# Aggregating x before the weights product: x stationary, the adjacency streamed 512 nodes wide, four tiles normed at once

## Chip, cores and metric

The kernel runs on one core of one Trainium2 chip. The metric is the device time of that core in microseconds (us); lower is better. Engines are named as in the profile: PE is TensorE (PEld its weight loads), DVE VectorE, ACT ScalarE, POOL GpSimd, SP the queue that issues most DMAs.

## What is computed

`x` is 4096 x 256, `adj` 4096 x 4096 (mostly zeros, with a full diagonal), `weight` 256 x 256, `t` one number, all fp32.

```python
support = x @ weight
g = (1.0 - t[0]) * support + t[0] * (adj @ support)
out = _layernorm(x + g, axis=-1)
```

Both kernels keep fp32 accuracy by splitting each operand into a high part (a copy rounded to the type fp32r) and a low part (the rest), and adding three products: high by high, high by low, low by high.

## The kernel before

**Support first.** x comes transposed in 16 chunks of 256 nodes (`x_raw`, a ring of 4). ACT makes `x_hi` (L168), POOL `x_lo` (L215). PE takes x as stationary and W as moving operand, 256 columns at a time: 6 matmuls for each of 32 tiles of 128 nodes, 192 in all (L331, L336, L341), into `s_ps`. ACT copies the result to the first 256 columns of `S[:, tile]` (L173) and DVE writes the rest to the last 256 (L247), so that S holds high and low side by side for all 4096 nodes.

**Aggregation.** The 32 output tiles go in 16 pairs. For a tile the transposed adjacency comes in two 1 MB chunks of 16 blocks (`a_raw`, a ring of 4). ACT makes `a_hi` (L180) and DVE `a_lo` (L253), 2048 elements a partition each. For each of the 32 blocks PE runs two matmuls with the adjacency block as the stationary operand: `a_hi` against all 512 columns of S (L361), and `a_lo` against its first 256 (L366). That is 1024 matmuls of each kind.

**Norm.** POOL forms `base` = (1 - t) S + x for a pair in three operations (L220, L223, L231). For each tile DVE adds both halves of `agg` to it (L260, L263) and takes statistics (L266, L270), ACT the root (L184), and DVE the reciprocal with one Newton step and `normed` (L274 to L287). The result is stored per tile.

**Order.** All engines run their own list in order and meet by semaphores. ACT: two `a_high`, then `root` of a tile. DVE: two `a_low`, then `layernorm`. SP: four `load_adj`, each after the `a_low` that frees its slot, `load_rows`, two stores. PE waits for `a_lo_ready` of a chunk, and for `y_ready` of the tile that used its accumulator before. The first matmul of the aggregation needs `S`.

Of the kernel before, what the change touches and what calls it, by code (L numbers as in the profile page):

```python
# [7 lines left out]
CHUNK_BLOCKS = 16  # L19
RING = 4  # L20
X_TILES = 2
X_RING = 4
# [3 lines left out]
def at_start(n):  # L26

    return isinstance(n, int) and n == 0

def gnn_layernorm_kernel(nc, xT, x, adjT, t, W, out):
# [3 lines left out]
    nodes, feats = x.shape  # L35
    TILES = nodes // P
    KT = feats // P
    CHUNK = CHUNK_BLOCKS * P
    PER_TILE = TILES // CHUNK_BLOCKS
    PAIRS = TILES // 2  # L40
    X_CHUNKS = TILES // X_TILES
    S_ROUNDS = X_CHUNKS // X_RING
    assert PER_TILE == 2 and RING == 2 * PER_TILE and S_ROUNDS <= RING

    ctx = ExitStack()
    with ctx:
# [9 lines left out]

# [3 lines left out]
        x_raw = sb("x_raw", [P, X_RING, KT, X_TILES * P])  # L60
        x_hi = sb("x_hi", [P, X_RING, KT, X_TILES * P], f32r)
        x_lo = sb("x_lo", [P, X_RING, KT, X_TILES * P], f32r)
        S = sb("S", [P, TILES, 2 * feats], f32r)
        a_raw = sb("a_raw", [P, RING, CHUNK])
        a_hi = sb("a_hi", [P, RING, CHUNK], f32r)
        a_lo = sb("a_lo", [P, RING, CHUNK], f32r)
        t_col = sb("t_col", [P, 1])
        omt_col = sb("omt_col", [P, 1])
        x_rows = sb("x_rows", [P, 2, feats])
        base = sb("base", [P, 2, feats])  # L70
        s_sum = sb("s_sum", [P, 2, feats])
        s_scaled = sb("s_scaled", [P, 2, feats])
        y_part = sb("y_part", [P, feats])
        y = sb("y", [P, feats])
        stats = sb("stats", [P, 6])
        mean_var = sb("mean_var", [P, 2])
        var_eps = sb("var_eps", [P, 1])
        std = sb("std", [P, 1])
        rstd0 = sb("rstd0", [P, 1])
        newton_q = sb("newton_q", [P, 1])  # L80
        newton_c = sb("newton_c", [P, 1])
        rstd = sb("rstd", [P, 1])
        normed = sb("normed", [P, 2, feats])

        s_ps = [ctx.enter_context(nc.psum_tensor(f"s_ps{i}", [P, X_TILES, feats], f32)) for i in range(X_RING)]
        agg = [ctx.enter_context(nc.psum_tensor(f"agg{i}", [P, 2 * feats], f32)) for i in range(2)]

        w_loaded, t_loaded = sem("w_loaded"), sem("t_loaded")  # L90
        w_hi_ready, w_lo_ready = sem("w_hi_ready"), sem("w_lo_ready")
        omt_ready = sem("omt_ready")
        x_loaded = sems("x_loaded", X_RING)
        x_hi_ready, x_lo_ready = sems("x_hi_ready", X_RING), sems("x_lo_ready", X_RING)
        s_acc_ready = sems("s_acc_ready", X_RING)
        s_hi_ready = sems("s_hi_ready", X_RING)
        s_lo_ready = sems("s_lo_ready", X_RING)
# [3 lines left out]
        rows_loaded = sem("rows_loaded")  # L101
        s_sum_ready, s_scaled_ready, base_ready = sem("s_sum_ready"), sem("s_scaled_ready"), sem("base_ready")
        y_part_ready = sem("y_part_ready")
        y_ready = sems("y_ready", 2)
        stats_ready, mean_var_ready = sem("stats_ready"), sem("mean_var_ready")
        var_eps_ready, std_ready, rstd0_ready = sem("var_eps_ready"), sem("std_ready"), sem("rstd0_ready")
        newton_q_ready, newton_c_ready = sem("newton_q_ready"), sem("newton_c_ready")
# [4 lines left out]

        @block.sync
        def _(sp):
            def load_x(chunk, slot):
                sp.dma_start(x_raw[:, slot], xT[bass.ds(chunk, 1)].rearrange("c p k n -> p (c k) n")
                             ).then_inc(x_loaded[slot], 16)

            def load_adj(chunk, slot):  # L120
                sp.dma_start(a_raw[:, slot], adjT[bass.ds(chunk, 1)].rearrange("c p n -> p (c n)")
                             ).then_inc(a_loaded[slot], 16)

            def load_rows(pair):
                sp.dma_start(x_rows[:, :, :], x[bass.ds(pair * (2 * P), 2 * P)].rearrange("(u p) f -> p u f", p=P)
                             ).then_inc(rows_loaded, 16)

            def store(pair, u):
                sp.wait_ge(normed_ready, pair * 2 + (u + 1))
                sp.dma_start(out[bass.ds(pair * (2 * P) + u * P, P)], normed[:, u]).then_inc(stored[u], 16)  # L130

            for slot in range(X_RING):
                load_x(slot, slot)
            sp.dma_start(t_col[:, :], t.partition_broadcast(P)).then_inc(t_loaded, 16)
            for r in range(1, S_ROUNDS):
                for slot in range(X_RING):
                    sp.wait_ge(x_lo_ready[slot], r)
                    load_x(r * X_RING + slot, slot)
                load_adj(r - 1, r - 1)
            for slot in range(S_ROUNDS - 1, RING):  # L140
                load_adj(slot, slot)
            load_rows(0)

            def refill(pair):
                for slot in range(RING):
                    sp.wait_ge(a_lo_ready[slot], pair + 1)
                    load_adj(pair * RING + (RING + slot), slot)
                sp.wait_ge(base_ready, pair + 1)
                load_rows(pair + 1)

            refill(0)
            with sp.Fori(1, PAIRS - 1) as pair:
                refill(pair)
                store(pair - 1, 0)
                store(pair - 1, 1)
            for pair in (PAIRS - 2, PAIRS - 1):
                store(pair, 0)
                store(pair, 1)
            for u in range(2):
                sp.wait_ge(stored[u], 16 * PAIRS)  # L160

        @block.scalar
        def _(act):
            def x_high(rnd, slot):
                act.wait_ge(x_loaded[slot], 16 * (rnd + 1))

                nc.scalar.activation(x_hi[:, slot], x_raw[:, slot], ACT.Copy).then_inc(x_hi_ready[slot], 1)  # L168

            def s_high(rnd, slot):  # L170
                act.wait_ge(s_acc_ready[slot], rnd + 1)
                tile = (rnd * X_RING + slot) * X_TILES
                nc.scalar.activation(S[:, bass.ds(tile, X_TILES), 0:feats], s_ps[slot][:, :, :], ACT.Copy  # L173
                                     ).then_inc(s_hi_ready[slot], 1)

            def a_high(rnd, slot):
                act.wait_ge(a_loaded[slot], 16 * (rnd + 1))
                if not at_start(rnd):
                    act.wait_ge(a_used[slot], rnd)
                nc.scalar.activation(a_hi[:, slot], a_raw[:, slot], ACT.Copy).then_inc(a_hi_ready[slot], 1)  # L180

            def root(tile):
                act.wait_ge(var_eps_ready, tile + 1)
# [3 lines left out]
            x_high(0, 0)  # L187
            act.wait_ge(w_loaded, 16)
            nc.scalar.activation(w_hi[:, :, :], w_raw[:, :, :], ACT.Copy).then_inc(w_hi_ready, 1)  # L189
            for slot in range(1, X_RING):  # L190
                x_high(0, slot)
            with act.Fori(0, S_ROUNDS - 1) as rnd:
                for slot in range(X_RING):
                    s_high(rnd, slot)
                    x_high(rnd + 1, slot)
            a_high(0, 0)
            for slot in range(X_RING):
                s_high(S_ROUNDS - 1, slot)
            for slot in range(1, RING):
                a_high(0, slot)  # L200
            with act.Fori(0, PAIRS - 1) as pair:
                for u in range(2):
                    a_high(pair + 1, 2 * u)
                    a_high(pair + 1, 2 * u + 1)
                    root(pair * 2 + u)
            root(TILES - 2)
            root(TILES - 1)

        @block.gpsimd  # L210
        def _(pool):
            with pool.Fori(0, S_ROUNDS) as rnd:
                for slot in range(X_RING):
                    pool.wait_ge(x_hi_ready[slot], rnd + 1)
                    nc.gpsimd.tensor_tensor(x_lo[:, slot], x_raw[:, slot], x_hi[:, slot].bitcast(f32), ALU.subtract  # L215
                                            ).then_inc(x_lo_ready[slot], 1)

            def make_base(pair):
                s_pair = S[:, bass.ds(pair * 2, 2), :].bitcast(f32)
# [8 lines left out]
                if not at_start(pair):  # L228
                    for u in range(2):
                        pool.wait_ge(y_ready[u], pair)  # L230
# [12 lines left out]
        def _(dve):  # L243
# [57 lines left out]
            for slot in range(1, RING):  # L301
                a_low(0, slot)
# [100 lines left out]
```

## Time and profile before

| | |
|---|---|
| median of 3 runs | 399.12 us (398.97 to 399.54) |
| span of the profiled execution | 397.6 us |
| what lies around the span, by these two | 1.5 us |
| PE busy | 384.0 us, 97% |
| DVE, ACT, POOL busy | 69%, 47%, 22% |
| HBM traffic | 80 MB, 201 GB/s over the span |

The profiled execution's own total is not shown apart from its span, so that the median stands in for it. A busy share is an average over the stages. PE is busy when a matmul is in it; ends of matmuls are modelled, so the spacing of starts is the better measure of what one costs.

### The profile page before, as it was taken

Reading aid. Unit: us, or ns where it says so; the run is one execution under the profiler, and the core shown is the slowest. Engines: PE = TensorE matmul, PEld = TensorE weight load, DVE = VectorE, ACT = ScalarE, POOL = GpSimd, SP = SyncE. Lnnn points to the kernel's source line nnn. Section 1 sums busy time; section 2 is a strip of 40 time slices with the busy share of each in tenths; the row PEclk is TensorE's granted clock in tenths of the full one; section 3 lists DMA queues with packets and bytes.
Section 4 is the critical chain, followed back from the end, with each engine's and each line's share of the span. In section 5 each row is a group of like instructions: output and inputs, shape, how many; then the busy total and the mean of one; then the engine's idle time right before and its main releaser. Section 6 shows DMA issues by size and latency. Waiting matters only on the chain.

```text
span 397.6 us, 6141 instructions
## 1 busy us (share of the span) xinstructions
PE 384.0 (97%) x2240; PEld 336.6 (85%) x2240; DVE 273.1 (69%) x402; ACT 185.1 (47%) x160; POOL 87.9 (22%) x68
## 2 busy tenths in 40 slices
PE   4989999999999999999999999999999999999994
PEld 3978888888888888888888888888888888888883
DVE  1438977777676767777676767777676767777622
ACT  5669535445452635445353635445353635445200
POOL 5765923030300203030200303030200303030100
PEclk9999999999999999999999999999999999999998
DMA  6996966675554665676554665675554664670000
GB/s 185 309 305 222 343 233 235 219 250 211 209 205 170 240 223 176 208 257 211 203 205 176 238 220 176 213 257 211 201 207 176 232 226 172 218 257 13 0 26 13
DMA packets 20900, 80.02 MB, mean 201 GB/s; under 512 B 2208, under 2 KB 10656, under 8 KB 12704
## 3 DMA queue, kind: packets, MB, share of 16 engines
q1 hardware_dynamic: 20624, 79.70, 57.0%
q10 hardware_dynamic: 272, 0.26, 0.2%
q8 instruction: 3, 0.05, 0.0%
q14 instruction: 1, 0.01, 0.0%
HBM read 75.76 MB, written 4.19 MB: 201 GB/s over the span
## 4 chain that ended last, share of the span: by engine, by line
PE 91%; DMA 4%; ACT 2%; DVE 2%; POOL 1%; issue 1%; ACTq 0%; DVEq 0%
PE agg L361 60%; PE agg L366 30%; DMA x_raw<-in_xT 4%; ACT x_hi L168 1%; POOL x_lo L215 1%; DVE a_lo L253 1%; ACT a_hi L180 0%; DVE w_lo L291 0%; PE s_ps L336 0%; ACT S L173 0%; PE s_ps L341 0%; ACT w_hi L189 0%; DVE y_part L260 0%; DVE y L263 0%; DVE stats L266 0%
## 5 line engine op out<-in xcount | busy, mean ns | idle before, releaser
L361 PE MATMUL agg<-S,a_hi 128*128 128x512 f32 x1024 | 356.4, 396 | 0.4 <-DVE a_lo L253 0.4
L366 PE MATMUL agg<-S,a_lo 128*128 128x256 f32 x1024 | 280.3, 279 | 0.0
L361 PEld LDWEIGHTS agg<-S,a_hi 128*128 128x128 f32 x1024 | 189.9, 188 | 44.0 <-DVE a_lo L253 0.6
L253 DVE TENSOR_TENSOR a_lo<-a_raw,a_hi 128x2048 fp32r<-128x2048 f32 x64 | 150.6, 2358 | 70.3 <-ACT a_hi L180 70.3
L366 PEld LDWEIGHTS agg<-S,a_lo 128*128 128x128 f32 x1024 | 192.9, 188 | 2.8
L180 ACT ACTIVATE a_hi<-a_raw 128x2048 fp32r<-128x2048 f32 x64 | 122.2, 1913 | 67.8 <-PE agg L361 67.7
L231 POOL TENSOR_TENSOR base<-s_scaled,x_rows 128x512 f32<-128x512 f32 x16 | 22.6, 1411 | 272.2 <-DVE y L263 272.1
L184 ACT ACTIVATE std<-var_eps 128x1 f32<-128x1 f32 x32 | 6.5, 203 | 126.1 <-DVE var_eps L272 126.1
L287 DVE TENSOR_SCALAR normed<-y,mean_var,rstd 128x256 f32<-128x256 f32 x32 | 24.5, 765 | 2.5
L220 POOL TENSOR_TENSOR s_sum<-S 128x512 f32 (+1 forms) x16 | 24.5, 1531 | 4.7 <-DVE S L247 4.7
L260 DVE SCALAR_TENSOR_TENSOR y_part<-agg,t_col,base 128x256 f32<-128x256 f32 x32 | 15.3, 478 | 11.2 <-PE agg L361 11.2
L215 POOL TENSOR_TENSOR x_lo<-x_raw,x_hi 128x512 fp32r<-128x512 f32 x16 | 20.7, 1314 | 10.0 <-ACT x_hi L168 9.5
L223 POOL TENSOR_TENSOR s_scaled<-s_sum,omt_col 128x512 f32<-128x512 f32 x16 | 20.5, 1282 | 1.3
L247 DVE TENSOR_TENSOR S<-s_ps,S 128x512 f32 (+1 forms) x16 | 10.8, 688 | 14.1 <-ACT S L173 14.1
L180 ACT ACT_TABLE_LOAD x15 | 19.2, 1283 | 2.5 <-issue 2.5
L331 PE MATMUL s_ps<-w_hi,x_hi 128*128 128x256 f32 x64 | 13.7, 297 | 6.5 <-ACT w_hi L189 5.5
L184 ACT ACT_TABLE_LOAD x15 | 19.2, 1283 | 0.3
L263 DVE SCALAR_TENSOR_TENSOR y<-agg,t_col,y_part 128x256 f32<-128x256 f32 x32 | 15.5, 484 | 1.1
L331 PEld LDWEIGHTS s_ps<-w_hi,x_hi 128*128 128x128 f32 x64 | 10.6, 204 | 6.7 <-ACT x_hi L168 6.7
L283 DVE TENSOR_TENSOR rstd<-newton_c,rstd 128x1 f32<-128x1 f32 x32 | 14.3, 447 | 1.1
L266 DVE BATCH_NORM_STATS2 stats<-y 128x6 f32<-128x256 f32 x32 | 13.7, 428 | 1.1
L341 PE MATMUL s_ps<-w_hi,x_lo 128*128 128x256 f32 x64 | 13.4, 293 | 0.6 <-POOL x_lo L215 0.6
(18 smaller groups left out, 87.1 us busy)
## 6 DMA issues: line engine op xcount, KB each, us to landing
a_raw<-in_adjT SPq DMA_DIRECT2D x64, 1024.0 KB, 4.8
x_raw<-in_xT SPq DMA_DIRECT2D x16, 256.0 KB, 4.3
x_rows<-in_x SPq DMA_DIRECT2D x16, 256.0 KB, 3.3
out<-normed SPq DMA_DIRECT2D x32, 128.0 KB, 1.7
w_raw<-in_W ACTq DMA_DIRECT2D x1, 256.0 KB, 4.0
t_col<-in_t SPq DMA_DIRECT2D x1, 0.5 KB, 4.2
```

What stands on the lines that cost most here:

```text
L180: nc.scalar.activation(a_hi[:, slot], a_raw[:, slot], ACT.Copy).then_inc(a_hi_ready[slot], 1)
L184: nc.scalar.activation(std[:, :], var_eps[:, :], ACT.Sqrt).then_inc(std_ready, 1)
L215: nc.gpsimd.tensor_tensor(x_lo[:, slot], x_raw[:, slot], x_hi[:, slot].bitcast(f32), ALU.subtract).then_inc(x_lo_ready[slot], 1)
L220: nc.gpsimd.tensor_tensor(s_sum[:, :, :], s_pair[:, :, 0:feats], s_pair[:, :, feats:2 * feats], ALU.add).then_inc(s_sum_ready, 1)
L223: nc.gpsimd.tensor_tensor(s_scaled[:, :, :], s_sum[:, :, :], omt_col[:, :].unsqueeze(2).broadcast_to([P, 2, feats]), ALU.mult).then_inc(s_ ...
L231: nc.gpsimd.tensor_tensor(base[:, :, :], s_scaled[:, :, :], x_rows[:, :, :], ALU.add).then_inc(base_ready, 1)
L253: nc.vector.tensor_tensor(a_lo[:, slot], a_raw[:, slot], a_hi[:, slot].bitcast(f32), ALU.subtract).then_inc(a_lo_ready[slot], 1)
L263: nc.vector.scalar_tensor_tensor(y[:, :], agg[u][:, feats:2 * feats], t_col[:, :], y_part[:, :], ALU.mult, ALU.add).then_inc(y_ready[u], 1)
L287: nc.vector.tensor_scalar(normed[:, u], y[:, :], mean_var[:, 0:1], rstd[:, :], ALU.subtract, ALU.mult).then_inc(normed_ready, 1)
L331: nc.tensor.matmul(s_ps[slot][:, h], x_hi[:, slot, k, cols], w_hi[:, k], start=(k == 0), stop=False)
L361: return nc.tensor.matmul(agg[u][:, :], a_hi[:, slot, cols], S[:, j], start=(j == 0), stop=(j == TILES - 1))
L366: return nc.tensor.matmul(agg[u][:, feats:], a_lo[:, slot, cols], S[:, j, 0:feats], start=False, stop=False)
```

## The change

The product is taken as (adj x) W instead of adj (x W).

- x comes untransposed (`x_sta`, 8 loads of 512 KB), and is split once into `x_hi` and `x_lo` for all nodes: 1024 elements a partition for each ACT and POOL operation. It is the stationary operand of the aggregation.
- The adjacency is the moving operand, 512 output nodes wide. There are 8 chunks of 512 output nodes; a chunk has 8 groups of 4 blocks of 128 source nodes; a group is one 1 MB load, one `a_high` and one `a_low` of the same size as before. A group is 4 blocks x 2 halves of the features x 3 products = 24 matmuls, all 512 columns wide, 1536 in all.
- The sum is transposed (features x nodes). DVE makes z = t * agg + (1 - t) * xT for the two halves (512 columns each), ACT `z_hi`, DVE `z_lo`. Then `project` multiplies with W: 6 matmuls of 256 columns for each of four tiles, 24 for a chunk, 192 in all. On PE `project(c - 1)` stands behind the first group of chunk c; on ACT and DVE z stands ahead of group 3, the norm behind group 4.
- DVE adds x's rows and takes statistics tile by tile; the small operations of the norm (root, reciprocal, Newton) work on four tiles at once. The last chunk's four tiles are stored one by one, other chunks in one store.
- POOL's three operations a pair go; it scales xT by (1 - t), once a chunk.
- The first group's load and split come in four parts. 9 matmuls on zeros stand ahead of the first real one (`WARM`). The activation table is loaded once at the start.
- Loops are unrolled: the program has no `Fori`.

```diff
+WIDE = 512
+GROUP = 4
+X_RING = 3
+WARM = 9
...
+        def y_tile(i):
+            return x_raw[:, 0, i]
+        def normed(c):
+            return x_raw[:, 1 + c % 2]
...
+            def load_x(g):
+                if g >= X_RING:
+                    sp.wait_ge(x_lo_ready, g - X_RING + 1)
...
+            load_x(0)
+            for b in range(GROUP):
+                landed = a0_loaded[b] if b < GROUP - 1 else a_loaded[0]
+                sp.dma_start(a_raw[:, 0, b], adjT[0, :, b]).then_inc(landed, 16)
...
+            for g in range(1, GROUPS):
+                load_x(g)
+                load_adj(0, g)
+            load_adj(1, 0)
+            load_xt(0)
             load_rows(0)
+            for c in range(1, CHUNKS):
+                for g in range(1, GROUPS):
+                    load_adj(c, g)
+                    if g == 2:
+                        load_xt(c)
+                    if g == 5:
+                        load_rows(c)
+                if c + 1 < CHUNKS:
+                    load_adj(c + 1, 0)
+                store(c - 1)
...
+            for c in range(1, CHUNKS):
+                for g in range(GROUPS):
+                    if g == RING - 1:
+                        z_high(c - 1)
+                    a_high(c, g)
+                    if g == RING:
+                        root(c - 1)
...
+            def make_z(c):
+                dve.wait_ge(xt_scaled, c + 1)
+                for k in range(KT):
+                    if k == 0:
+                        dve.wait_ge(agg0_ready, c + 1)
+                    else:
+                        dve.wait_ge(a_used[RING - 1], turn(c, GROUPS - 1) + 1)
...
+                    nc.vector.scalar_tensor_tensor(z[:, k], agg[c % 2][k][:, :], t_col[:, :], xt[:, c % 2, k],
+                                                   ALU.mult, ALU.add).then_inc(z_ready[k], 1)
+                for k in range(KT):
+                    dve.wait_ge(z_hi_ready[k], c + 1)
...
+                    nc.vector.tensor_tensor(z_lo[:, k], z[:, k], z_hi[:, k].bitcast(f32), ALU.subtract
+                                            ).then_inc(z_lo_ready[k], 1)
...
+            def products(c, slot, j, b, k, first, last):
+                bank = agg[c % 2][k][:, :]
+                cols = slice(k * P, (k + 1) * P)
+                nc.tensor.matmul(bank, x_hi[:, j, cols], a_hi[:, slot, b], start=first, stop=False)
+                nc.tensor.matmul(bank, x_hi[:, j, cols], a_lo[:, slot, b], start=False, stop=False)
+                return nc.tensor.matmul(bank, x_lo[:, j, cols], a_hi[:, slot, b], start=False, stop=last)
...
+            def project(c):
+                for k in range(KT):
+                    pe.wait_ge(z_lo_ready[k], c + 1)
+                for i in range(TILES):
+                    if c:
+                        pe.wait_ge(y_ready[i], c)
+                    cols = slice(i * P, (i + 1) * P)
+                    dst = out_ps[i][:, 0:feats]
+                    for k in range(KT):
+                        nc.tensor.matmul(dst, z_hi[:, k, cols], w_hi[:, k], start=(k == 0), stop=False)
+                        nc.tensor.matmul(dst, z_hi[:, k, cols], w_lo[:, k], start=False, stop=False)
+                        done = nc.tensor.matmul(dst, z_lo[:, k, cols], w_hi[:, k], start=False, stop=(k == KT - 1))
+                    done.then_inc(prod_ready[i], 1)
+
+            pe.wait_ge(zeros_ready, 1)
+            for _ in range(WARM):
+                nc.tensor.matmul(out_ps[0][:, :], z_hi[:, 0, 0:P], z_hi[:, 0], start=True, stop=True)
+            first_group()
+            for g in range(1, GROUPS):
+                group(0, g)
+            pe.wait_ge(w_lo_ready, 1)
+            for c in range(1, CHUNKS):
+                group(c, 0)
+                project(c - 1)
+                for g in range(1, GROUPS):
+                    group(c, g)
+            project(CHUNKS - 1)
```

## Rows read from the trace of the kernel before

**Rows 1.** The page, part 1: busy us (share of the span) xinstructions.

```profile
PE 384.0 (97%) x2240; PEld 336.6 (85%) x2240; DVE 273.1 (69%) x402; ACT 185.1 (47%) x160; POOL 87.9 (22%) x68
```

**Rows 2.** The page, part 4: the chain that ended last, by engine.

```profile
PE 91%; DMA 4%; ACT 2%; DVE 2%; POOL 1%; issue 1%; ACTq 0%; DVEq 0%
```

**Rows 3.** Windows: stretch, length, busy of each engine, granted clock, DMA share, GB/s.

```profile
0.00:10.00 10.00, 4.11 (x20) 3.85 (x21) 1.37 (x2) 5.13 (x8) 5.36 (x8) 1.00 0.64 184
...
100.00:200.00 100.00, 100.00 (x573) 87.05 (x572) 71.81 (x108) 47.27 (x36) 17.86 (x15) 1.00 0.61 213
```

**Rows 4.** The chain in order of time: the marks at tile boundaries (start, us, what).

```profile
44.69 0.47 PE agg L361 x2
55.78 0.46 PE agg L361 x2
67.08 0.47 PE agg L361 x2
```

**Rows 5.** Timeline of PE at a tile boundary: start, us, engine, line, operation, count.

```profile
66.92 0.63 PE L361 MATMUL agg<-S,a_hi 128*128 128x512 f32 x2
67.38 0.39 PE L366 MATMUL agg<-S,a_lo 128*128 128x256 f32 x2
67.61 0.40 PE L361 MATMUL agg<-S,a_hi 128*128 128x512 f32 x1
```

**Rows 6.** Timeline of PE in the support stage, early and once under way.

```profile
7.25 0.63 PE L341 MATMUL s_ps<-w_hi,x_lo 128*128 128x256 f32 x2
...
7.68 0.63 PE L331 MATMUL s_ps<-w_hi,x_hi 128*128 128x256 f32 x2
...
10.03 0.40 PE L336 MATMUL s_ps<-w_lo,x_hi 128*128 128x256 f32 x2
...
10.27 0.40 PE L341 MATMUL s_ps<-w_hi,x_lo 128*128 128x256 f32 x2
```

**Rows 7.** Groups by line and shape: busy us, mean ns of one, idle before, releaser.

```profile
L253 DVE TENSOR_TENSOR a_lo<-a_raw,a_hi 128x2048 fp32r<-128x2048 f32 x64 | 150.6, 2358 | 70.3 <-ACT a_hi L180 70.3
L180 ACT ACTIVATE a_hi<-a_raw 128x2048 fp32r<-128x2048 f32 x64 | 122.2, 1913 | 67.8 <-PE agg L361 67.7
...
L215 POOL TENSOR_TENSOR x_lo<-x_raw,x_hi 128x512 fp32r<-128x512 f32 x16 | 20.7, 1314 | 10.0 <-ACT x_hi L168 9.5
...
L168 ACT ACTIVATE x_hi<-x_raw 128x512 fp32r<-128x512 f32 x16 | 10.0, 628 | 7.0 <-DMA x_raw<-in_xT 7.0
...
L247 DVE TENSOR_TENSOR S<-s_ps,S 128x512 f32 x12 | 8.3, 692 | 14.1 <-ACT S L173 14.1
```

**Rows 8.** Timeline of DVE while POOL runs too.

```profile
35.62 15.23 DVE L253 TENSOR_TENSOR a_lo<-a_raw,a_hi 128x2048 fp32r<-128x2048 f32 x5
```

**Rows 9.** Timeline of POOL in the same stretch.

```profile
35.87 3.19 POOL L220 TENSOR_TENSOR s_sum<-S 128x512 f32<-128x512 f32 x1 [4.71 <-DVE S L247]
```

**Rows 10.** Timeline of ACT at the start.

```profile
4.08 0.63 ACT L168 ACTIVATE x_hi<-x_raw 128x512 fp32r<-128x512 f32 x1 [1.55 <-DMA x_raw<-in_xT]
```

**Rows 11.** DMA from 10 to 34 us: packets, MB, share of 16 engines.

```profile
q1 hardware_dynamic: 2273, 7.06, 85.8%
```

**Rows 12.** The same from 34 to 60 us.

```profile
q1 hardware_dynamic: 1211, 7.08, 75.6%
```

**Rows 13.** Window of 395 to 396 us, columns as in rows 3.

```profile
395.00:396.00 1.00, 0.00 (x0) 0.00 (x0) 0.43 (x2) 0.00 (x0) 0.00 (x0) 0.50 0.00 0
```

**Rows 14.** Timeline of the end, from the last matmul.

```profile
391.52 0.40 PE L361 MATMUL agg<-S,a_hi 128*128 128x512 f32 x1
391.95 0.48 DVE L260 SCALAR_TENSOR_TENSOR y_part<-agg,t_col,base 128x256 f32<-128x256 f32 x1 [7.59 <-PE agg L361]
...
392.99 0.43 DVE L266 BATCH_NORM_STATS2 stats<-y 128x6 f32<-128x256 f32 x1
393.52 0.18 DVE L270 BATCH_NORM_AGGREGATE mean_var<-stats 128x2 f32<-128x6 f32 x1
...
393.93 0.20 ACT L184 ACTIVATE std<-var_eps 128x1 f32<-128x1 f32 x1 [10.90 <-DVE var_eps L272]
...
395.05 0.41 DVE L287 TENSOR_SCALAR normed<-y,mean_var,rstd 128x256 f32<-128x256 f32 x1
```

More of the change, by code:

```diff
@@ L59, in gnn_layernorm_kernel @@
         w_lo = sb("w_lo", [P, KT, feats], f32r)
[L60 to L66, printed above, removed]
+        x_raw = sb("x_raw", [P, X_RING, GROUP, feats])
+        x_hi = sb("x_hi", [P, BLOCKS, feats], f32r)
@@ L67, in gnn_layernorm_kernel @@
+        x_lo = sb("x_lo", [P, BLOCKS, feats], f32r)
+        a_raw = sb("a_raw", [P, RING, GROUP, WIDE])
+        a_hi = sb("a_hi", [P, RING, GROUP, WIDE], f32r)
+        a_lo = sb("a_lo", [P, RING, GROUP, WIDE], f32r)
+        xt = sb("xt", [P, 2, KT, WIDE])
+        rows = sb("rows", [P, 2, TILES, feats])
+        z = sb("z", [P, KT, WIDE])
+        z_hi = sb("z_hi", [P, KT, WIDE], f32r)
+        z_lo = sb("z_lo", [P, KT, WIDE], f32r)
         t_col = sb("t_col", [P, 1])
         omt_col = sb("omt_col", [P, 1])
-        x_rows = sb("x_rows", [P, 2, feats])
@@ L83, in gnn_layernorm_kernel @@
[L83 to L92, printed above, removed]
+        stats = sb("stats", [P, TILES, 6])
+        mean_var = sb("mean_var", [P, TILES, 2])
@@ L111, in gnn_layernorm_kernel, with turn @@
         block = ctx.enter_context(nc.Block())
+        def turn(c, g):
+            return 2 * c + g // RING
         @block.sync
         def _(sp):
[L116 to L133, printed above, removed]
-            sp.dma_start(t_col[:, :], t.partition_broadcast(P)).then_inc(t_loaded, 16)
@@ L135, in _ @@
[L135 to L141, printed above, removed]
-            load_rows(0)
[L144 to L160, printed above, removed]
+            def load_x(g):
+                if g >= X_RING:
+                    sp.wait_ge(x_lo_ready, g - X_RING + 1)
+                sp.dma_start(x_raw[:, g % X_RING], x_sta[:, g * GROUP:(g + 1) * GROUP]
+                             ).then_inc(x_loaded[g % X_RING], 16)
@@ L163, in _ @@
+            for i in range(TILES):
+                c = CHUNKS - 1
+                sp.wait_ge(normed_ready, c * TILES + i + 1)
+                sp.dma_start(out[c * WIDE + i * P:c * WIDE + (i + 1) * P], normed(c)[:, i]
+                             ).then_inc(stored[c % 2], 16)
+            sp.wait_ge(stored[0], 16 * (CHUNKS // 2))
+            sp.wait_ge(stored[1], 16 * (CHUNKS // 2 - 1 + TILES))
         @block.scalar
         def _(act):
-            def x_high(rnd, slot):
-                act.wait_ge(x_loaded[slot], 16 * (rnd + 1))
-                nc.scalar.activation(x_hi[:, slot], x_raw[:, slot], ACT.Copy).then_inc(x_hi_ready[slot], 1)
@@ L182, in root, with x_high, a_high @@
-            def root(tile):
-                act.wait_ge(var_eps_ready, tile + 1)
+            def x_high(g):
+                act.wait_ge(x_loaded[g % X_RING], 16 * (g // X_RING + 1))
+                nc.scalar.activation(x_hi[:, g * GROUP:(g + 1) * GROUP], x_raw[:, g % X_RING], ACT.Copy
+                                     ).then_inc(x_hi_ready, 1)
+            def a_high(c, g):
+                slot = g % RING
+                act.wait_ge(a_loaded[slot], 16 * (turn(c, g) + 1))
+                if turn(c, g):
+                    act.wait_ge(a_used[slot], turn(c, g))
+                nc.scalar.activation(a_hi[:, slot], a_raw[:, slot], ACT.Copy).then_inc(a_hi_ready[slot], 1)
@@ L188, in _ @@
[L188 to L207, printed above, removed]
+            act.preload_act_table_set("sqrt_and_others")
+            x_high(0)
+            for b in range(GROUP):
+                act.wait_ge(a0_loaded[b] if b < GROUP - 1 else a_loaded[0], 16)
+                nc.scalar.activation(a_hi[:, 0, b], a_raw[:, 0, b], ACT.Copy
+                                     ).then_inc(a0_hi_ready if b < GROUP - 1 else a_hi_ready[0], 1)
@@ L210, in _ @@
+            z_high(CHUNKS - 1)
+            root(CHUNKS - 1)
         @block.gpsimd
         def _(pool):
[L212 to L219, printed above, removed]
[L220 to L232 removed]
@@ L234, in _, with x_low @@
-            pool.wait_ge(omt_ready, 1)
-            for slot in range(X_RING):
-                pool.wait_ge(s_lo_ready[slot], S_ROUNDS)
-            make_base(0)
-            with pool.Fori(1, PAIRS) as pair:
-                make_base(pair)
+            def x_low(g):
+                pool.wait_ge(x_hi_ready, g + 1)
+                nc.gpsimd.tensor_tensor(x_lo[:, g * GROUP:(g + 1) * GROUP], x_raw[:, g % X_RING],
+                                        x_hi[:, g * GROUP:(g + 1) * GROUP].bitcast(f32), ALU.subtract
+                                        ).then_inc(x_lo_ready, 1)
@@ L242, in _ @@
+            for c in range(CHUNKS):
+                scale_xt(c)
         @block.vector
         def _(dve):
[L244 to L249 removed]
@@ L310, in _ @@
-            pair_of_tiles(0)
-            with dve.Fori(1, PAIRS - 1) as pair:
-                pair_of_tiles(pair)
-            layernorm(PAIRS - 1, 0)
-            layernorm(PAIRS - 1, 1)
+                dve.wait_ge(rstd_ready, c + 1)
+                if c >= 2:
+                    dve.wait_ge(stored[c % 2], 16 * (c // 2))
+                for i in range(TILES):
+                    nc.vector.tensor_scalar(normed(c)[:, i], y_tile(i), mean_var[:, i, 0:1], rstd[:, i:i + 1],
+                                            ALU.subtract, ALU.mult).then_inc(normed_ready, 1)
@@ new lines, in group @@
+            def group(c, g):
+                slot = g % RING
+                pe.wait_ge(a_lo_ready[slot], turn(c, g) + 1)
+                if c == 0:
+                    pe.wait_ge(x_lo_ready, g + 1)
+                for k in range(KT):
+                    if c >= 2 and g == 0:
+                        pe.wait_ge(z_ready[k], c - 1)
+                    for b in range(GROUP):
+                        j = g * GROUP + b
+                        done = products(c, slot, j, b, k, j == 0, j == BLOCKS - 1)
+                    if g == GROUPS - 1 and k == 0:
+                        done.then_inc(agg0_ready, 1)
+                done.then_inc(a_used[slot], 1)
```

312 lines of the change are left out of this document (144 added, 168 removed).

## The prediction

> **What bounds the kernel now.** The page's first part says that PE is busy for 97% of the span [rows 1], and the chain says that 91% of the span is PE work [rows 2]. The windows show where the rest is: in the first 10 us PE works 4.11, from 100 to 200 us it works all of the time [rows 3]. So three things can move the end: how long the first microseconds keep PE waiting, what the matmuls cost, and what follows the last of them.
>
> For the second the busy time is no help, because matmuls overlap; I read the spacing of starts. Marks of the chain at three tile boundaries lie 11.09 and 11.30 us apart [rows 4]. A tile is 32 pairs of a 512- and a 256-column matmul, so a pair takes 0.3466 or 0.3531 us, mean 0.3498. At a boundary two wide matmuls follow each other, then two narrow ones: the wide two take 67.38 - 66.92 = 0.46 us, the narrow two 67.61 - 67.38 = 0.23 [rows 5]. So a wide one costs 0.23 and a narrow one 0.115, wherever it stands. The trace has 31 such boundaries; the wide two take 0.46 in 15 of them and 0.47 in 16, as in [rows 4], so 0.2328 each. The support stage, narrow only, has two in 0.24 (10.03 to 10.27), 0.120 each; earlier two take 0.43 (7.25 to 7.68), 0.215 each [rows 6]. That spacing is 256 columns at the 1.2 GHz level (213 ns), although the windows give a granted clock of 1.00 there [rows 3]; the later one is the 2.4 GHz level (107 ns) plus 9 to 13 ns.
>
> **Matmuls: the sum.** The number of columns does not change. Before: 1024 x (512 + 256) = 786,432 for the aggregation and 192 x 256 = 49,152 for the weights. After: 1536 x 512 = 786,432, and again 192 x 256. Only their grouping does: 2048 matmuls become 1536. What this is worth hangs on whether the 8 or 9% above the bare columns is paid per matmul or per column. The starts of [rows 5] say per column: 0.23 against 0.115, in two neighbours of the same kind. I bound the price of a wide matmul from both sides. Below: the quicker pair less the dearer narrow one, 0.3466 - 0.120 = 0.2266. Above: the slower pair less 0.118, 0.235. Between: mean pair less 0.115 to 0.120 is 0.230 to 0.235, and the boundaries give 0.2328. I take 0.2325. The 1512 wide matmuls of groups 1 to 63 are then 351.5 us, and the ends are 342.6 and 355.3. All 1536 are 357.1, where the old aggregation took 1024 x 0.3498 = 358.2: the core of the change gains 1 us. `project` costs the same 192 x 0.120 = 23.0 us as before.
>
> **The start.** Before, the first x chunk is there at 4.08 us [rows 10], when 0.52 MB (x and W, 256 KB each) had been moved. The DMA moved 7.06 MB in 24 us at a share of 0.858, and 7.08 in 26 at 0.756 [rows 11, 12]: 343 and 360 GB/s when in use, so about 350. The transfers then began at about 4.05 - 0.52/0.35 = 2.55. After, the first x load is 512 KB and lands 0.75 later, at 4.8. `x_hi` of 1024 columns is between 0.628 and 1.913 [rows 7], by interpolation 1.05: 5.85. `x_lo` of 1024 is twice 1.314 [rows 7], 2.6; but while DVE ran `a_lo` a POOL operation of 512 took 3.19 us and DVE needed 15.23/5 = 3.05 for an `a_lo` [rows 8, 9] that else takes some 2.3. DVE's small `a_lo` parts of the first group fall into it, so I take 3.0: PE begins at 8.9, where before it began at 5.5. The 9 matmuls on zeros lie in this wait and cost nothing; they end near 5 (9 x 0.43), and about 3 us after the last matmul the old kernel was granted 0.50 [rows 13, 14], so the first group may start at half speed again. It ends at 8.9 + 24 x 0.2325 = 14.5, or some 1.8 later.
>
> Group 1 then waits for data. Up to its end 0.26 (W) + 0.52 + 1.05 + 0.52 + 1.05 = 3.41 MB must be in: 2.55 + 3.41/0.35 = 12.3. `a_hi` 1.91 and `a_lo` 2.3 [rows 7] come on top: 16.6. That hides the slow clock. From there a group costs PE 24 x 0.2325 = 5.58, DMA 1.57/0.35 = 4.5, ACT 1.05 + 1.91, DVE 2.36 and POOL 2.6 to 5. PE is the slowest, and stays in work. SP's waits in this stage (`load_x` for the third `x_lo` before, `load_adj` for `a_low`) are over before the queue has drained.
>
> **The chunks.** z of a chunk is made behind its last matmul, and PE meanwhile has group 0 of the next one, 5.58 us. The chain is z 0.75 (a read of 512 PSUM columns, L247 took 0.69 [rows 7]), `z_hi` 0.63, `z_lo` 0.6 and gaps: 2.3 us. It is hidden, with 3 us to spare; without that cover it would cost 7 x 2.3 = 16 us. Behind `make_z` on DVE and `z_high` on ACT stands group 3, needed on PE at 5.58 + 2.88 + 11.2 = 19.6 us into the chunk; it is split by 6. The norm of four tiles stands on DVE behind group 4 (from 9.7 to about 18), and ACT's `root` holds `a_high` of group 5 until 15. Group 5 is split by 20 and needed at 31. SP's store waits until 18 and holds only loads whose slots come free after 20. All this costs nothing. POOL has one scaling of 2.6 to 6 us a chunk. DMA needs per chunk 8.4 + 1.6 MB in 47.5 us, 210 GB/s, as before. The 30 table loads that go were off the chain.
>
> **The end.** Here the change adds. Before: 391.52 to 397.6, of which 0.23 is the last matmul [rows 14]. After its slot: 0.20 until DVE may read; the z chain 2.1; first tile of `project` 0.95 (five starts at 0.12 and the modelled end); four times y and statistics, 4 x 1.02 = 4.1 (0.48 and 0.43 with their gaps); four aggregates 0.8; the small chain with the root 1.4; four `normed` of 0.41 with gaps, 1.7; the store as before, 397.6 - 395.46 = 2.14, and 0.1 for SP's four issues: 13.5. Before it was 5.85, so this adds 7.6.
>
> **Sum.** 16.6 + 351.5 + 7 x 24 x 0.120 (20.2) + 13.5 = 401.8 us span, against 397.6. With the 1.5 that the median of the runs lies above the profiled span: **403.3 us**, 1% slower. By parts: start +1, matmuls -1, projection in the end -2.9 (24 of 192 are counted there), end +7.6.
>
> **Rivals.**
> 1. *The toll is per matmul.* For: 0.120 - 0.1067 is 13.3 ns, and (346.6 - 320)/2 is 13.3 too, so one fixed toll fits the support stage and the quicker pair. Against: the starts in [rows 5]. It gives 0.2267 a wide matmul, 8.8 us less: 394.5, faster. The sign turns at 1512 x d = 4.2, a price of 0.2297.
> 2. *A uniform wide stream has no toll* (the other side, far out): what is paid is the meeting of weight loads with 256-column matmuls, which leaves too little time to hide a load; the loads' busy time is 85% [rows 1]. Then 0.2135 (half of two times 0.2135, the 1.2 GHz spacing of 256): 28.7 less, 374.6. Against: two wide ones in a row cost 0.46. The Trainium skill's rule above lies near it.
> 3. *The slow tiles are the rule*: 0.235 or more because what the other engines and the DMA do slows the stream: +3.8, 407.
> 4. *The start is DMA-bound or the clock is low longer.* Chunk 0 needs 1.57 MB per 5.58 us, 282 GB/s. If it gets 250, each of 7 groups takes 0.7 more, +5: 408. The opposite, a first group that is not held by group 1's data, gives back at most 2.
>
> **Chances.** My forecast (400 to 407, rival 3 among it) 0.52; above 407 0.06; rival 1 (392 to 397) 0.20; rival 2 (372 to 382) 0.12; between 397 and 400 0.10. A difference under 0.2% (398.3 to 399.9) can't be told from no change; that makes faster 0.36, same 0.08, slower 0.56. The range takes in rival 1 and the contended price with the slow start, 393 to 408, and leaves rival 2 out. The likeliest case by itself: 400 to 407.
>
> **What would show it.** Spacing of wide matmuls in the middle of the stream: 0.231 to 0.235 if I am right, 0.227 for rival 1, 0.214 to 0.216 for rival 2. Group 1 begins at 16 to 17 us. No PE waits from there to the last chunk, and none before `project`. From the last wide matmul to the end 13 to 14 us. The forecast fails if the wide price is below 0.230, or if PE shows gaps within a chunk.

## The result and the profile after

The changed kernel takes **395.8 us** (median of 7 runs, 395.5 to 397.25) against 399.12 (7 runs, 398.0 to 399.6). The ratio is 0.9922, 95% interval 0.9903 to 0.9941: 0.8% faster. I had forecast 403.3 and slower. The profiled execution took 395.5 with a span of 393.7, so 1.8 lie around the span, as in all 7 runs; the forecast of the span was 401.8.

The first part of the page after, to be held against [rows 1]:

```profile
PE 379.0 (96%) x1737; PEld 315.7 (80%) x1737; DVE 227.7 (58%) x277; ACT 143.8 (37%) x101; POOL 46.9 (12%) x21
```

The other engines have become idler, PE has not: it is still what sets the time. The chain in order of time has a mark at the first group of each chunk behind `project` (start, us, what), three of them here as in [rows 4]:

```profile
111.10 0.23 PE agg L324
...
157.52 0.23 PE agg L324
...
203.94 0.23 PE agg L324
```

A chunk takes 46.42 us in these two intervals and in the three behind them. Less `project` at 24 x 0.120 = 2.88, that is 43.54 for 192 wide matmuls: **0.2268 each**, not 0.2325. The timeline of PE in the middle of the stream says the same, six starts in 1.36 us:

```profile
149.73 0.39 PE L324 MATMUL agg<-a_hi,x_hi 128*128 128x512 f32 x1
149.95 0.39 PE L325 MATMUL agg<-a_lo,x_hi 128*128 128x512 f32 x1
150.18 0.39 PE L326 MATMUL agg<-a_hi,x_lo 128*128 128x512 f32 x1
...
151.09 0.39 PE L324 MATMUL agg<-a_hi,x_hi 128*128 128x512 f32 x1
```

The starts over the whole trace give each group of 24 a length of 5.44 us (0.2267), with few exceptions: the group behind each `project` takes 5.47, and where PE has waited for data (groups 1 and 3 of the first chunk) it takes 5.61. In group 1 the second matmul starts 0.34 behind the first, the next ten lie 0.22 to 0.24 apart, and the rest of the group runs at 0.2267.

**Where the time went**, from spans (-3.9) and starts of the two traces:

| part | before | after | difference |
|---|---|---|---|
| aggregation on PE, waits in it apart | 358.4 | 348.2 | -10.2 |
| slower groups after waits and `project`, and the wait at group 3 | | 1.1 | +1.1 |
| start, without PE's useful work | 33.36 - 23.0 = 10.3 | 17.17 - 5.44 = 11.7 | +1.4 |
| `project` that stands in the stream | 23.0 | 20.2 | -2.9 |
| from the last wide matmul's end on | 5.85 | 12.55 | +6.7 |

The end, to be held against [rows 14]: the timeline from the last z on.

```profile
381.35 0.75 DVE L249 SCALAR_TENSOR_TENSOR z<-agg,t_col,xt 128x512 f32<-128x512 f32 x1 [1.91 <-PE agg L326]
382.01 1.47 DVE L255 TENSOR_TENSOR z_lo<-z,z_hi 128x512 fp32r<-128x512 f32 x2
...
383.59 0.36 PE L365 MATMUL out_ps<-w_hi,z_hi 128*128 128x256 f32 x1 [2.28 <-DVE z_lo L255]
...
384.64 0.42 DVE L264 TENSOR_TENSOR x_raw<-out_ps,rows 128x256 f32<-128x256 f32 x1 [1.15 <-PE out_ps L367]
...
385.44 0.41 DVE L264 TENSOR_TENSOR x_raw<-out_ps,rows 128x256 f32<-128x256 f32 x1
...
387.79 0.36 DVE L270 BATCH_NORM_AGGREGATE mean_var<-stats 128x2 f32<-128x6 f32 x4
...
389.64 1.38 DVE L289 TENSOR_SCALAR x_raw<-x_raw,mean_var,rstd 128x256 f32<-128x256 f32 x4
390.08 1.80 SPq L157 DMA_DIRECT2D out<-x_raw  x4
```

PE stands still for 2.28 us while z is made, tiles follow each other on DVE every 0.79 us on average, the small operations run once for all four (387.79 to 389.64), and SP issues four stores in a row.

And the start: DVE and POOL in the first chunk, where PE's only wait behind group 1 arises. Group 3 begins at 28.83, when the first of the four `a_lo` in the last DVE row is done.

```profile
18.60 2.94 DVE L236 TENSOR_TENSOR a_lo<-a_raw,a_hi 128x2048 fp32r<-128x2048 f32 x1 [1.48 <-ACT a_hi L174]
21.46 2.89 DVE L303 TENSOR_TENSOR w_lo<-w_raw,w_hi 128x512 fp32r<-128x512 f32 x1
...
24.34 17.68 DVE L236 TENSOR_TENSOR a_lo<-a_raw,a_hi 128x2048 fp32r<-128x2048 f32 x4
```
```profile
16.34 3.04 POOL L214 TENSOR_TENSOR x_lo<-x_raw,x_hi 128x1024 fp32r<-128x1024 f32 x1 [2.54 <-ACT x_hi L166]
19.59 7.04 POOL L214 TENSOR_TENSOR x_lo<-x_raw,x_hi 128x1024 fp32r<-128x1024 f32 x2 [0.20 <-ACT x_hi L166]
27.13 12.74 POOL L214 TENSOR_TENSOR x_lo<-x_raw,x_hi 128x1024 fp32r<-128x1024 f32 x3 [0.50 <-ACT x_hi L166]
```

Four `a_lo` take 17.68 us, 4.4 each, while POOL works on `x_lo`. By itself an `a_lo` takes 2.3 and an `x_lo` of this size 2.3 (the one from 5.77 on), and 4.4 is close to the sum. The single rows fit turns, one whole instruction after the other: the `a_lo` from 18.60 ends 2.2 us behind POOL's end at 19.38, and `w_lo` from 21.46, which takes 2.89, ends 0.5 us behind POOL's next end at 23.81. No run changes this alone.

### The profile page after: what moved, and what is told of

It is laid out like the page before. It is cut to its first block, busy times and chain, and to the rows that moved or that the text cites. A ratio compares the mean times of both kernels' runs of the same rounds, so it can differ in the third digit from the quotient of the medians.

```text
span 393.7 us, 4192 instructions
## 1 busy us (share of the span) xinstructions
PE 379.0 (96%) x1737; PEld 315.7 (80%) x1737; DVE 227.7 (58%) x277; ACT 143.8 (37%) x101; POOL 46.9 (12%) x21
## 4 chain that ended last, share of the span: by engine, by line
PE 90%; DVE 4%; DMA 3%; SPq 1%; issue 1%; ACT 1%; DVEq 0%
PE agg L324 28%; PE agg L326 28%; PE agg L325 28%; DMA a_raw<-in_adjT 3%; DVE a_lo L236 2%; PE out_ps L365 2%; PE out_ps L367 2%; PE out_ps L366 2%; DVE w_lo L303 1%; ACT a_hi L174 0%; SPq L136 0%; DVE x_raw L264 0%; SPq L107 0%; DVE x_raw L289 0%; DVE z_lo L255 0%
## 5 line engine op out<-in xcount | busy, mean ns | idle before, releaser
L324 PE MATMUL agg<-a_hi,x_hi 128*128 128x512 f32 x512 | 200.6, 392 | 4.1 <-DVE a_lo L297 3.3
L325 PE MATMUL agg<-a_lo,x_hi 128*128 128x512 f32 x512 | 200.3, 391 | 0.0
L326 PE MATMUL agg<-a_hi,x_lo 128*128 128x512 f32 x512 | 200.0, 391 | 0.0
L324 PEld LDWEIGHTS agg<-a_hi,x_hi 128*128 128x128 f32 x512 | 96.7, 189 | 25.5 <-issue 3.9
L326 PEld LDWEIGHTS agg<-a_hi,x_lo 128*128 128x128 f32 x512 | 96.7, 189 | 20.2
L325 PEld LDWEIGHTS agg<-a_lo,x_hi 128*128 128x128 f32 x512 | 96.7, 189 | 19.9
L220 POOL TENSOR_TENSOR xt<-xt,omt_col 128x1024 f32<-128x1024 f32 x8 | 18.6, 2324 | 261.6 <-DMA xt<-in_xT 261.6
L214 POOL TENSOR_TENSOR x_lo<-x_raw,x_hi 128x1024 fp32r<-128x1024 f32 x8 | 27.5, 3457 | 11.1 <-ACT x_hi L166 11.1
L365 PE MATMUL out_ps<-w_hi,z_hi 128*128 128x256 f32 x64 | 18.1, 284 | 2.3 <-DVE z_lo L255 2.3
L367 PE MATMUL out_ps<-w_hi,z_lo 128*128 128x256 f32 x64 | 18.1, 283 | 0.0
```

The source lines that it names most:

```text
L214: nc.gpsimd.tensor_tensor(x_lo[:, g * GROUP:(g + 1) * GROUP], x_raw[:, g % X_RING], x_hi[:, g * GROUP:(g + 1) * GROUP].bitcast(f32), ALU.s ...
L220: nc.gpsimd.tensor_tensor(xt[:, c % 2], xt[:, c % 2], omt_col[:, :].unsqueeze(2).broadcast_to([P, KT, WIDE]), ALU.mult).then_inc(xt_scaled, 1)
L324: nc.tensor.matmul(bank, x_hi[:, j, cols], a_hi[:, slot, b], start=first, stop=False)
L325: nc.tensor.matmul(bank, x_hi[:, j, cols], a_lo[:, slot, b], start=False, stop=False)
L326: return nc.tensor.matmul(bank, x_lo[:, j, cols], a_hi[:, slot, b], start=False, stop=last)
L365: nc.tensor.matmul(dst, z_hi[:, k, cols], w_hi[:, k], start=(k == 0), stop=False)
```

## Experiments

**1. Is the toll per matmul or per column?** In the changed kernel each wide matmul but the 16 that open an accumulation is cut in two:

```diff
...
+                    for h in range(2):
+                        half = slice(h * 256, (h + 1) * 256)
+                        done = nc.tensor.matmul(agg[c % 2][k][:, half], sta[:, j, cols], mov[:, slot, b, half],
+                                                start=False, stop=last and n == 2 and h == 1)
...
```

> The changed kernel with 1520 of its 1536 wide matmuls taken as two of 256 columns each (same stationary block, same columns in all). Fixed toll per matmul of 13.3 ns (rival 1): two narrow ones cost 0.240 us where a wide one cost 0.2267, 1520 x 0.0133 = 20 us more, span about 414; narrow starts 0.120 apart, a group 5.76 us. Toll per column (my forecast's assumption): the groups stay at 5.44 us and the span at 394.

Measured: 416.55 us (4 runs), ratio to the kernel before 1.0431 (1.0383 to 1.0479). That is 20.75 over the changed kernel; the fixed toll said 20.2, the toll per column nothing. The last wide product begins 19.9 later than in the changed kernel (400.85 against 380.92). Another 1.2 us of the profiled run are a fall of the clock in the last `project`, which experiment 4 is about. The timeline of PE (two matmuls a row), and two marks of the chain one chunk apart:

```profile
200.14 0.40 PE L329 MATMUL agg<-a_hi,x_hi 128*128 128x256 f32 x2
200.38 0.40 PE L329 MATMUL agg<-a_lo,x_hi 128*128 128x256 f32 x2
```
```profile
107.45 0.24 PE agg L325
...
156.40 0.24 PE agg L325
```

0.240 for the pair where 0.2267 was the price of the same columns at once. A chunk takes 48.95 in place of 46.42, 2.53 for 190 matmuls more, 13.3 ns each. So each matmul costs its columns at 2.4 GHz and 13.3 ns. Each of these matmuls comes with a weight load of its own, so this does not say whether load or matmul is what the 13.3 ns are for.

**2. What made half of the old tiles slow?** The fixed toll gives 0.3467 for a pair and 11.09 for a tile. The kernel before has that in every second tile only. Three kernels made from it: PE's loop over pairs written out (`b_unroll`), one order in all blocks (`b_order`), the two accumulators' banks exchanged (`b_banks`).

```diff
-            with pe.Fori(1, PAIRS) as pair:
+            for pair in range(1, PAIRS):
                 adj_round(pair)
```

> The kernel before with only PE's loop over the pairs written out, so that no branch or register operation stands between matmuls. Half of its tiles take 11.30 us and half 11.09. If the loop makes the slow ones, all tiles but perhaps the first take 11.09 and the time falls by 15 x 0.21 = 3.2 us. If it is the accumulator's bank or an order of matmuls, the two lengths stay and the time is the same within 0.3 us.

```diff
...
-                            if j == 0:
-                                high()
-                                last = low()
-                            else:
-                                low()
-                                last = high()
+                            high()
+                            last = low()
```

> The kernel before with one order in all blocks of the aggregation, wide then narrow, so that no two wide and no two narrow ones follow each other at a tile's start (before, block 0 is wide, narrow and the others are narrow, wide). If the pair of equals at the boundary flips PE between a quick and a slow rhythm, all tiles get one length: 11.30 (+3.3 us in all) or 11.09 (-3.3 us). If bank or loop decides, tiles still alternate between 11.30 and 11.09 and the time stays.

```diff
-        agg = [... for i in range(2)]
+        agg = [... for i in range(2)][::-1]
```

> The kernel before with the two accumulators' PSUM banks exchanged. If the bank makes a tile slow, the slow tiles become the odd ones (11.09 and 11.30 exchange places; the last tile, quick before, takes 11.30). If loop or order does, nothing changes.

`b_unroll`: 398.32 (10 runs), ratio 0.9985 (0.9966 to 1.0003), and its marks still alternate: the loop is not it. `b_banks` (one run, 398.19) turned it round; in its chain the interval that was 11.09 and then 11.30 in [rows 4] is 11.29 and then 11.10:

```profile
43.03 0.46 PE agg L361 x2
54.32 0.47 PE agg L361 x2
65.42 0.46 PE agg L361 x2
```

That looked like the bank. But `b_order` took 402.32 (6 runs), ratio 1.0092 (1.0063 to 1.0121), and its tiles take 11.30 in both banks (the first 11.40). So the bank does not make a tile slow. I then put both edits together:

> The kernel before with one order of matmuls in all blocks, and the two accumulators' banks exchanged. With one order all tiles took 11.30. If the slow rhythm belongs to the order (wide, narrow from the start on), all take 11.30 again, span about 399.7. If the exchange of banks (after which tile 0 was quick and the odd ones slow) sets which rhythm the stream starts in, all take 11.09, span about 393.

Its one run took 397.01, with 11.09 for each tile behind the first. Timed again:

> The same kernel as in the single look (one order of matmuls in all blocks, banks exchanged), now timed. All of its 31 later tiles took 11.09 there, against 11.30 with the banks as they were. If the exchange sets the rhythm, every run is near 397 and the ratio to the kernel before about 0.994, to the one without the exchange 0.986. If the rhythm was chance, runs spread between 396 and 402.5, or the median is near 402.

The four runs took 403.48, 403.17, 403.39 and 395.82. The windows of 100 to 200 us, first of `b_order_banks`, then of the profiled run of the same kernel in the timed series; columns as in [rows 3], where the kernel before has x573:

```profile
100.00:200.00 100.00, 100.00 (x579) 87.41 (x578) 72.46 (x109) 47.45 (x36) 17.93 (x15) 1.00 0.60 214
```
```profile
100.00:200.00 100.00, 100.00 (x568) 86.82 (x567) 71.14 (x107) 45.40 (x35) 16.63 (x14) 1.00 0.58 206
```

The same program runs at 0.3467 or at 0.3532 a pair from end to end, with the same granted clock. The two executions read here took 397.01 and 403.48, 6.5 us apart, which is 31 x 0.21. The run of 395.82 has no trace; by its time it belongs to the quick rhythm. So the expectation that the banks set it is refuted. What the runs show: an alternation of wide and narrow has two rhythms; which one a stream begins in differs from run to run; it keeps it while the order is uniform. In the kernel before, with two equal ones side by side at each tile's start, the length changes at every one of its tiles, so that it always pays half, 16 x 0.21 = 3.4 us. In the changed kernel, wide only, starts above 0.2267 last for half a group after a wait and are gone. Why a stream falls into one or the other stays open.

**3. The norm of four tiles at once**, undone alone:

```diff
...
-                dve.wait_ge(mean_var_ready, (c + 1) * TILES)
-                nc.vector.tensor_scalar(var_eps[:, :], mean_var[:, :, 1], EPS, None, ALU.add).then_inc(var_eps_ready, 1)
+                    dve.wait_ge(mean_var_ready, n)
+                    nc.vector.tensor_scalar(var_eps[:, one], mean_var[:, i, 1:2], EPS, None, ALU.add
+                                            ).then_inc(var_eps_ready, 1)
...
```

> The changed kernel with the norm's small operations (aggregate, root, reciprocal, Newton step, normed) done tile by tile again, and not on four tiles at once. In the stream DVE and ACT have room, so nothing there. At the end each tile is a serial chain of about 3.1 us (as 391.95 to 395.46 less one of two adds in the kernel before), four of them 12.4 where the joint form takes 6.4; the stores then overlap better by up to 1. Expected +5 us (span about 398.7). If the joint form were worth nothing: 0 to +1.

Measured: 400.39 (10 runs), ratio 1.0041 (1.0026 to 1.0057), 4.6 us over the changed kernel. The stream keeps its 5.44 us a group; at the end the tiles start 2.85 apart (384.90, 387.76, 390.61, 393.46 on DVE). The clock fell in the last `project` of this profile too, but the first tile starts 1.06 behind the first matmul of it, as in the changed kernel (1.05), and what holds the others is DVE's own list. Without this part the change as a whole would have been a loss.

**4. The start: matmuls on zeros**, none in place of 9, and 18.

```diff
-WARM = 9
+WARM = 0      # the other kernel: 18
```

> The changed kernel without the 9 matmuls on zeros. They end about 5.5 us and the first real one starts at 8.77 with wide starts 0.427 apart until 13.6, so they gave no quick start; group 1 begins when its data are split (17.2). Expected: first group at the same spacing, group 1 at the same time, span within 0.3 us of 393.7. If they do matter: group 0 slow for longer, group 1 later by up to 1 us.

> The changed kernel with 18 matmuls on zeros in place of 9, so that they reach up to the first real one. If an unbroken stream is what the quick clock needs, group 0 has wide starts 0.23 apart from its beginning and ends at about 14.6 in place of 16.6; group 1 still begins at 17.2, since its split data are what it waits for, and the span stays at 393.7 (within 0.3). If the first real one is held back by them, +0.5.

One run each, 396.87 and 398.0 us, where I had expected no change of the span beyond 0.3. Without them the first group has the same slow spacing as with 9 (timeline of PE):

```profile
9.43 0.63 PE L325 MATMUL agg<-a_lo,x_hi 128*128 128x512 f32 x1
9.85 0.63 PE L326 MATMUL agg<-a_hi,x_lo 128*128 128x512 f32 x1
10.28 0.63 PE L324 MATMUL agg<-a_hi,x_hi 128*128 128x512 f32 x1
```

0.427 each, 512 columns at the 1.2 GHz level with no toll on top. With 18:

```profile
9.45 0.39 PE L325 MATMUL agg<-a_lo,x_hi 128*128 128x512 f32 x1
9.68 0.40 PE L326 MATMUL agg<-a_hi,x_lo 128*128 128x512 f32 x1
9.91 0.40 PE L324 MATMUL agg<-a_hi,x_hi 128*128 128x512 f32 x1
```

0.23 from the first. The profile of `a_pertile`, with 9, shows what comes between: the granted clock is 1.00 from 5.8 to 9.0 and 0.50 from 9.3 to 12.5, behind 3.2 us in which PE did nothing; with 18 that pause is 1.24. (For the changed kernel the windows give 1.00 from 9 to 13 us, where starts are 0.427 apart; the starts decide.) And neither moves group 1 much: it begins at 17.27 and 17.69, when its data are split (17.17 in the changed kernel, 17.43 in `a_pertile` and 17.54 in `a_bridge`, all with 9). The last group begins its last matmul at 380.97 and 381.40 (380.92). Yet their spans are 395.1 and 395.4, 1.4 and 1.7 more, and that led to the end of the kernel. Timeline of PE in the last `project`, first of the changed kernel, then of the one without zeros:

```profile
383.78 0.28 PE L366 MATMUL out_ps<-w_lo,z_hi 128*128 128x256 f32 x1
383.90 0.28 PE L367 MATMUL out_ps<-w_hi,z_lo 128*128 128x256 f32 x1
```
```profile
383.85 0.41 PE L366 MATMUL out_ps<-w_lo,z_hi 128*128 128x256 f32 x1
384.06 0.42 PE L367 MATMUL out_ps<-w_hi,z_lo 128*128 128x256 f32 x1
384.27 0.41 PE L365 MATMUL out_ps<-w_hi,z_hi 128*128 128x256 f32 x1
```

The windows of 384 to 388 us of the same two; the granted clock is the last but two:

```profile
384.00:388.00 4.00, 2.70 (x23) 2.49 (x21) 3.23 (x11) 0.00 (x0) 0.00 (x0) 1.00 0.00 0
```
```profile
384.00:388.00 4.00, 4.00 (x24) 4.00 (x22) 2.13 (x5) 0.00 (x0) 0.00 (x0) 0.60 0.00 0
```

While z of the last chunk is made PE stands still for 2.3 us; in some runs the clock then falls to the 1.2 GHz level for most of the 24 narrow matmuls, DVE waits for them, and the end is 1.2 to 1.3 us later. The changed kernel itself probably has it both ways: five of its 7 runs take 395.5 to 395.9 at a mean granted clock of 0.994 to 0.995, two 397.2 at 0.986. Those two have no trace.

**5. PE kept at work through that gap:**

```diff
+            pe.wait_ge(y_ready[TILES - 1], CHUNKS - 1)
+            for _ in range(9):
+                nc.tensor.matmul(out_ps[TILES - 1][:, :], x_hi[:, 0, 0:P], a_hi[:, 0, 0], start=True, stop=True)
             project(CHUNKS - 1)
```

> The changed kernel with 9 wide matmuls of no use between its last group and the last project, so that PE works through the 2.3 us in which z of the last chunk is made. In three of four profiles of variants the 24 narrow matmuls of that project have starts 0.21 apart for most of the way, in the changed kernel's own 0.12. If the gap is what lets the clock fall, the spacing is 0.12 in every run and the spread of the times goes to its quick end: median 395.5 or just under, no run near 397. If the clock falls for another reason, the 0.21 comes up again; if the extra ones hold project up, +0.3.

Measured: 395.79 (4 runs, 395.71 to 396.01), ratio 0.9917 (0.9898 to 0.9935). The spacing is 0.12 in its profile, and no run lies near 397; four runs are few for a thing that happened in two of seven, so I call it in line with the expectation. The profiles say more than the "three of four" above: in all five variants without these 9 (`a_split`, `a_pertile`, `a_warm0`, `a_warm18`, `a_best`) the last `project` has 15 or 16 of its 24 matmuls at the slow spacing, and in both with them none. The median does not move.

**6. A better version.** The start of the stream hangs on data: group 1 waits for its `a_lo`, group 3 for an `a_lo` behind which W's split stood on DVE (2.89 us while POOL was busy). Four edits at the ends (`a_best`), and the 9 matmuls of experiment 5 on top (`a_best2`):

```diff
+WARM = 18
...
+                    nc.scalar.activation(a_hi[:, 1, 0:2], a_raw[:, 1, 0:2], ACT.Copy).then_inc(a1_hi_ready, 1)
+                    nc.scalar.activation(a_hi[:, 1, 2:4], a_raw[:, 1, 2:4], ACT.Copy).then_inc(a_hi_ready[1], 1)
...
-                if g == 2:
+                if g == 6:
                     dve.wait_ge(w_hi_ready, 1)
...
+            for i in range(1, TILES, 2):
+                act.wait_ge(normed_ready, c * TILES + i + 1)
+                act.dma_start(out[c * WIDE + i * P:c * WIDE + (i + 1) * P], normed(c)[:, i]
...
```

> The changed kernel with four edits at its ends: 18 matmuls on zeros, group 1's split in two halves with their own signals, W's split moved behind group 6 of the first chunk on DVE, and the last four stores issued from two queues. Stream unchanged at 5.44 us a group. Start: group 1 at about 15, group 2 at 21.5 (its data), group 3 at 27 in place of 28.8, so -1.9; end: -0.6 from the stores. Span about 391.2, time about 393.0. If the clock falls anyway or DVE is too slow beside POOL in the first chunk, the start gives only the 0.6 of W's move, and the span is 392.5.

> The four edits at the ends (18 matmuls on zeros, group 1 split in halves, W's split later, last stores from two queues) together with the 9 wide ones ahead of the last project. The last group ends at 379.3 as before these; with project's starts 0.12 apart the rest takes 12.2 in place of 13.5: span 391.5, time 393.3 (394.7 without the 9). If the gap does not matter, 394.7 again.

`a_best`: 394.68 (6 runs), ratio 0.9888 (0.9861 to 0.9915), where 393.0 was expected. Group 1 begins at 15.98, group 2 at 21.56, group 3 at 27.13, the last matmul 1.87 us sooner than in the changed kernel; but its profiled run has the slow last `project`, so the span is 392.8. `a_best2`: **394.1** (4 runs, 393.43 to 394.42), ratio 0.9872 (0.985 to 0.9893), span 391.8, `project` at 0.12. It beats both kernels, 1.3% under the kernel before; its interval does not meet that of the changed kernel. What 0.6 between the last two is worth, the runs leave within their spread. Stores from two queues gave 0.3 and not 0.6: from the last wide matmul's end on it is 12.24 in `a_best2` and 12.58 in `a_bridge`.

One thing eats part of the gain. In every run of the changed kernel and of its variants with 0 or 9 matmuls on zeros the time is 1.8 or 1.9 above the span; in the 11 runs with 18 (`a_warm18`, `a_best`, `a_best2`) it is 2.1 to 3.3. `a_warm18` differs from the changed kernel in nothing else and has 2.6. Why is open, and `a_best2` with 9 was not run. By spans `a_best2` is 2.5 us ahead of the changed kernel (391.2 to 391.8 against 393.7 to 394.1 in its quick runs), by medians 1.7.

## Why the prediction was wrong

- **The step that failed** is the price of the wide matmul, "the boundaries give 0.2328. I take 0.2325". It measured 0.2267, and 1512 x 0.0058 = 8.8 us is more than the whole error of the span, 8.1. The mechanism was wrong with it: I read the starts as a toll per column, and it is a toll of 13.3 ns per matmul. It was my rival 1, with its number: the bound from below, to which I gave 0.20. Experiment 1 shows it. The other errors of the sum nearly cancel: +0.6 for group 1's start, +1.1 for slow groups and group 3's wait, -0.95 for the end.
- Why the reading misled: I took the distance between two starts for the price of the first. In a change of widths the starts shift by some nanoseconds from wide to narrow (0.234 and 0.116 on average in the trace before, where 0.2267 and 0.120 are what each costs in a row of its own kind; in the quick rhythm alone, `b_order_banks`, 0.2318 and 0.1150), and half of the tiles ran in the slow rhythm, which the new stream does not stay in. The two wide ones at a boundary are two matmuls in a mix, not a uniform stream. The 0.118 in the bound from above stands there without a row behind it; it did no harm. What would have served was in the text too: 13.3 ns came out of the narrow stage and out of the quicker pair, two stretches that knew nothing of each other.
- **"The core of the change gains 1 us"**: it gains 10.2. Of it 512 x 13.3 ns = 6.8 are matmuls that are no longer there, and 3.4 the slow rhythm.
- **The rule of the Trainium skill** ("TensorE: Matmul & The Clock Gate", "Back-to-back issue gap"), columns at 2.4 GHz plus 2.5 ns, which the page gives for the isolated gap of a single matmul, does not hold here: 512 columns measured 226.7 ns, 256 columns 120. The row was the better guide, though the rule has the form right: a fixed part for each matmul. Rival 2, a stream with no toll, fell with it.
- **The start** was right in its mechanism: PE's first matmul at 8.77 (8.9), slow spacing until 13.6, group 1 held by its `a_lo` until 17.17 (16.6). "PE is the slowest, and stays in work" missed one wait: group 3, 28.83. DVE's `a_lo` beside POOL took 2.9 to 4.5 and W's split, which I had not put in this sum, 2.9. With the slow groups after waits that is 1.1 us. `a_best` has W's split behind group 6, and its group 3 follows group 2 without a wait.
- **The chunks** were right: no wait of PE from group 3 of the first chunk to the last, none before a `project`.
- **The end** measured 12.55 for 13.5. The y and statistics of a tile took 0.79 and not 1.02, the four aggregates 0.36 and not 0.8, since operations that do not wait for each other overlap by some 0.1 us; the stores took 0.4 more, four issues of 0.45 in a row on SP. I had put the clock's fall into the first group; in the end, where it costs 1.2 to 1.3 us, I had not.
- **Around the span** I added 1.5, the median less the span of another run. Taken run by run it is 1.9 or 2.0 for the kernel before and 1.8 for the changed one.
- The range held the time, since it took in rival 1; the sign did not hold: slower had 0.56, faster 0.36.

## What to carry to other kernels

Take the price of an instruction from a period that repeats and contains a known number of them, and solve for the parts with a second stretch of another mix; the distance of two neighbours in a mix is not it. When two independent stretches give the same fixed toll, that is stronger than a spacing read at 10 ns. Regrouping the same columns into fewer matmuls is worth the toll times their number, and work that moves to the serial end of a kernel has to be set against it.

## What the hardware showed that I had not expected

- An fp32r matmul with its weight load costs its columns at 2.4 GHz and 13.3 ns (0.120 us for 256, 0.2267 for 512), at 1.2 GHz the bare columns (0.427 for 512).
- An alternation of 512 and 256 columns has two stable rhythms, 0.3467 and 0.3532 us a pair; the same program was read in both, at 397.0 and at 403.5 us, at the same granted clock.
- After 2.3 us in which PE did nothing the clock fell during the 24 matmuls behind in five profiles and not in a sixth; 9 matmuls in the gap went with the full clock in both profiles that had them.
- DVE and POOL hold each other up when both split operands: `a_lo` took 4.4 us where it takes 2.3 alone, `w_lo` (512 elements a partition) 2.89. In the kernel before `w_lo` ran beside POOL too and took 1.22, from 5.38 on: POOL's `x_lo` of 1.26 from 4.79 on ended 0.55 before it. By these rows an instruction pays the rest of the other one, and that depends on when it comes.
